# Steps moved off VectorE in a four-layer kernel, and the ranks of its order set anew

## What is computed

```python
# 1: selective scan, 256 channels, 32 states
delta = softplus(x @ W_bc[:64].T @ W_dt.T + b_dt);  B, C = x @ W_bc[64:96].T, x @ W_bc[96:].T
h[t] = exp(delta[t] * A) * h[t-1] + delta[t] * x[t] * B[t];   y[t] = sum_n h[t] * C[t] + D * x[t]
# 2: dense FFN, 704 hidden, weights (wq - 128) * scale
y = (silu(x @ Wg.T) * (x @ Wu.T)) @ Wd.T
# 3: convolution of 4 taps and scan, 512 channels, 16 states
hs = silu(conv4(x @ W_in.T) + conv_b);  delta = softplus((hs @ W_dt.T) @ W_dtproj.T + b)
y = (scan(hs, delta, B, C) + D * hs) * silu(x @ W_gate.T) @ W_out.T
# 4: causal attention, 16 heads of 128; experts, the best 6 of 16, and a shared one
x4 = x + softmax(q k^T / sqrt(128) + mask) v @ wo          # q, k, v from rmsnorm(x) * ln1
y  = x4 - x + sum_e cw[e] * (silu(h @ eg[e].T) * (h @ eu[e].T)) @ ed[e].T + shared(h)  # h: rmsnorm(x4) * ln2
```

## Time and profile before

| | us |
|---|---|
| median of 3 runs | 1362.71 |
| lowest, highest | 1359.16, 1363.14 |
| profiled execution, its own time | 1363.67 |
| its span, first to last instruction | 1362.4 |
| PE, DVE busy | 1119.7, 1030.9 |
| ACT, POOL busy | 596.2, 600.4 |

### The profile page before, as it was taken

One profiled execution on the slowest core, in us unless ns is written; L12 is line 12 of the kernel. 1 busy time (PEld: TensorE's weight loads), 2 busy tenths in 40 slices (PEclk: granted clock), 3 DMA queues, 4 the chain that ended last, 5 costly groups with the idle time before them and its releaser, 6 DMA issues. The chain is left out here.

```text
span 1362.4 us, 17002 instructions
## 1 busy us (share of the span) xinstructions
PE 1119.7 (82%) x5224; PEld 879.8 (65%) x5224; DVE 1030.9 (76%) x1879; ACT 596.2 (44%) x1543; POOL 600.4 (44%) x487
## 2 busy tenths in 40 slices
PE   4557536499695899977977899799998999999797
PEld 2335324377584678755855787587877877777586
DVE  5797899989999999999997885699944444444433
ACT  4553555454664336555753232565532123333210
POOL 3577477964575687654875640176600000000000
PEclk9798758899797999998988999899999999999899
DMA  4652124353254775433765641266543643222173
GB/s 135 251 195 74 48 88 142 108 158 105 85 174 155 218 232 166 136 101 111 210 216 156 196 144 43 83 201 199 162 144 104 204 136 104 95 93 81 58 210 103
DMA packets 105434, 191.54 MB, mean 141 GB/s; under 512 B 11648, under 2 KB 42368, under 8 KB 105088
## 3 DMA queue, kind: packets, MB, share of 16 engines
q1 hardware_dynamic: 91520, 177.42, 41.9%
q10 hardware_dynamic: 13824, 13.05, 3.1%
HBM read 176.33 MB, written 14.09 MB: 140 GB/s over the span
## 5 line engine op out<-in xcount | busy, mean ns | idle before, releaser
L1957 DVE TENSOR_TENSOR_SCAN scan_banks<-scan_banks,h_end,drive 128x256 f32<-128x256 f32 x480 | 338.5, 742 | 13.9 <-POOL drive L2291 11.0
L2321 POOL TENSOR_TENSOR sum<-sum,state 128x512 f32<-128x512 f32 x174 | 227.3, 1306 | 54.4 <-DVE state L1969 52.3
L2291 POOL TENSOR_TENSOR drive<-w0T,bc_rows 128x512 f32<-128x512 f32 x128 | 164.3, 1291 | 152.0 <-DVE scan_banks L1957 98.0
L2291 POOL TENSOR_TENSOR drive<-w1T,bc_rows 128x512 f32<-128x512 f32 x128 | 163.4, 1283 | 139.6 <-DVE scan_banks L1957 61.4
L2324 POOL TENSOR_TENSOR stats_b<-stats_b,neg_half 128x2 f32<-128x2 f32 x12 | 8.8, 732 | 367.4 <-DVE stats_b L2129 200.8
L1969 DVE TENSOR_TENSOR state<-scan_banks,bc_rows 128x512 f32<-128x512 f32 x240 | 162.7, 678 | 0.6
L1410 PE MATMUL score_banks<-state,ident 128*128 128x256 f32 x256 | 85.2, 483 | 79.3 <-DVE state L1969 44.7
L1560 PE MATMUL score_banks<-kv,qT 128*128 128x512 f32 (+3 forms) x360 | 135.7, 493 | 6.4 <-ACT probs L1865 3.7
L2144 DVE TENSOR_REDUCE soft<-score_banks 128x1 f32<-128x128 f32 (+4 forms) x122 | 88.0, 729 | 61.9 <-PE score_banks L1562 61.6
L1865 ACT ACTIVATE probs<-score_banks,soft 128x128 f32<-128x128 f32 (+4 forms) x122 | 87.8, 721 | 97.5 <-DVE soft L2144 96.7
L1410 PEld LDWEIGHTS score_banks<-state,ident 128*128 128x128 f32 x256 | 57.2, 239 | 107.5 <-DVE state L1969 57.4
(11 more groups left out here) (203 smaller groups left out, 2098.6 us busy)
## 6 DMA issues: line engine op xcount, KB each, us to landing
bc_rows<-bc_rows SPq DMA_DIRECT2D x256, 256.0 KB, 3.8
streamed_w<-in_w_head SPq DMA_DIRECT2D x64, 384.0 KB, 5.0
expert_w<-in_w_moe SPq DMA_DIRECT2D x52, 384.0 KB, 4.4
kv_past<-kv ACTq DMA_DIRECT2D x48, 256.0 KB, 3.2
kv<-in_w_moe SPq DMA_DIRECT2D x32, 384.0 KB, 3.9
kv<-kv_past SPq DMA_DIRECT2D x16, 768.0 KB, 4.7
kv<-kv_past SPq DMA_DIRECT2D x16, 512.0 KB, 5.0
streamed_w<-in_w_moe SPq DMA_DIRECT2D x16, 384.0 KB, 4.1
```

Source lines behind the costliest of these rows:

```text
L1957: done = e.engine.tensor_tensor_scan(states, decays, drive[g % len(drive)][:, i, 0:size], h_end[layer][:, n, kt:kt + 1], ALU.mult, ALU.add)
L2291: self.tt(drive[g % len(drive)][:, :, 0:size], w_of(layer, c)[:, PAIR * half:PAIR * (half + 1), 0:size], rows_of(g, c, 0), ALU.mult).then_ ...
L2321: self.tt(to, so_far, slot_of(c, layer, k), ALU.add).then_inc(added, 1)
```

## The change

Parts of stages are handed to other engines, and the planner's numbers are new.

- `softplus_sum` keeps two instructions on DVE (minimum and last sum). cs, e - cs and plus max(x, 0) go to POOL (`softplus_rest`), `w` too (`delta_x`). `softplus_log` is split into `softplus_exp` and `softplus_log`. The half in layer 1's `w` goes into the weights that make B (scale 0.25 for 0.5).
- The first tap of the convolution goes from DVE to ACT, 16 instructions in all; `rms_scale` goes from DVE to ACT, 16.
- `weigh_up` of chunks 0 and 1 goes from DVE to POOL, 22 instructions.
- `on_scalar`: all groups of chunks 0 and 1, and groups 0 and 2 of chunk 2 are copied by ACT (before: group 1 of each); chunk 3 as before.
- The costs of `pe`, `pe_turn` and of transfers, the lags, `EARLIER` and the lanes' ranks are new, and with them the order on every engine.

```diff
-    return "pe", sum(0.018 + 0.00172 * n for n in columns)
+    return "pe", sum(0.012 + 0.00169 * n for n in columns)
-DMA = "sp", 0.3
+def dma(kilobytes):
+    return "sp", max(0.5, kilobytes / 230)
...
-        return [Lane(self.fetches(), 0.00, 1), Lane(self.decays(), 0.60), Lane(self.drives(), 0.30), Lane(self.scans(), 0.10),
+        return [Lane(self.fetches(), 2.10, 1), Lane(self.decays(), 0.70), Lane(self.drives(), 0.10), Lane(self.scans(), -0.80),
...
-    return j == 2 if c == LAST else j % 2 == 1
+    return j == 2 if c == LAST else c < 2 or j != 1
...
             def softplus_sum(self, c, g):
-                self.ts(cs, es, 1.0, -1.0, ALU.add, ALU.add).then_inc(*self.order.tick())
+                e.wait_ge(sp_one[layer], c, half)
                 e.wait_ge(sp_ln[layer], c, half)
-                self.settle()
                 self.tt(ls, ls, cs, ALU.min).then_inc(*self.order.tick())
-                self.tt(cs, es, cs, ALU.subtract).then_inc(*self.order.tick())
-                self.tt(cs, cs, xs, ALU.add).then_inc(*self.order.tick())
+                e.wait_ge(sp_rest[layer], c, half)
-                self.tt(to, cs, ls, ALU.add).then_inc(delta_ready[layer].sem, 1)
-                    self.stt(to_w, hs[:, 2 * half:2 * half + 2, 0:size], 0.5, to, ALU.mult,
-                             ALU.mult).then_inc(w_ready[1].sem, 1)
-                    self.tt(to_w, to, x0s[c % 2][:, :, 0:size], ALU.mult).then_inc(w_ready[0].sem, 1)
+                self.tt(to, lost, ls, ALU.add).then_inc(delta_ready[layer].sem, 1)
...
+            def softplus_rest(self, c, g):                       # GpSimd
+                e.wait_ge(sp_exp[layer], c, half)
+                self.ts(cs, es, 1.0, -1.0, ALU.add, ALU.add).then_inc(sp_one[layer].sem, 1)
+                e.wait_ge(sp_one[layer], c, half)
+                wait_unit(e, driven, c - 1 if layer else c - 2, layer)
+                self.tt(lost, es, cs, ALU.subtract).then_inc(sp_lost[layer].sem, 1)
+                e.wait_ge(sp_lost[layer], c, half)
+                e.wait_ge(sp_x[layer], c, 2 * half + 1)
+                self.tt(lost, lost, xs, ALU.add).then_inc(sp_rest[layer].sem, 1)
+            def delta_x(self, c, g):                             # GpSimd
+                e.wait_ge(delta_ready[layer], c, half)
+                self.tt(to, of, x, ALU.mult).then_inc(w_ready[layer].sem, 1)
...
+            def conv_taps(self, c, kt):                          # ScalarE
+                self.activation(hs[:, kt, 0:size], pad_hs[:, kt, 0:size], ACT.Identity, bias=col("conv_b", kt),
+                                scale=col("conv_w", kt * TAPS)).then_inc(conv_begun.sem, 1)
...
+            def rms_scale(self, c, r):                           # ScalarE
+                    done = self.activation(hn[:, tb, :], x[:, tb, :], ACT.Copy, scale=st[:, tb, 2:3])
...
+            def weigh_up(self, c, g):                            # GpSimd, c < WEIGHED_BY_POOL = 2
+                self.tt(by_tile(to, size), by_tile(to, size), cw_rows[cw_at(c, r)][:, 0:len(GROUPS[g]), 0:size],
+                        ALU.mult).then_inc(moe_weighed.sem, 1)
```

More of the change, by code:

```diff
@@ L170, in nothing @@
         pass
-    load = load_x = dbc = project_dt = softplus_abs = softplus_x = softplus_log = softplus_sum = chore = nothing
+    load = load_x = dbc = project_dt = softplus_abs = softplus_x = softplus_exp = softplus_rest = softplus_log = softplus_sum = delta_x = chore = nothing
     fetch = decay = drive = scan = weigh = carry = add_up = skip0 = skip1 = nothing
@@ L298, in fetches @@
             after = ((f"rows{layer}", c),) + ((("weigh", g - ROWS),) if g >= ROWS else ())
-            yield Stage(partial(self.p.fetch, g, c, layer, k), (DMA,), after, (("rows", g),), lag=3.0)
+            yield Stage(partial(self.p.fetch, g, c, layer, k), (dma(SIZES[c]),), after, (("rows", g),), lag=2.4)
     def each(self):
@@ L328, in drives @@
             g, c, layer, k = unit
-            after = [("delta", c, 0 if layer == 0 else 1 + k // STATE1), ("rows", g)]
+            after = [("w", c, 0 if layer == 0 else 1 + k // STATE1), ("rows", g)]
             if g >= DRIVES:
@@ L415, in lanes @@
     def lanes(self):
-        return [Lane(self.first(), 0.20, 8), Lane(self.second(), 1.30, 16)]
+        return [Lane(self.first(), -0.30, 8), Lane(self.second(), 1.00, 16)]
     def softplus(self, c, g, given, use):
@@ L519, in load_lane @@
     for i in range(len(LOADS)):
-        yield Stage(partial(p.load, i), (DMA,), (("scan", i + 1),), (("in", i),), lag=10.0)
+        yield Stage(partial(p.load, i), (dma(LOADED_KB[i]),), (("scan", 2 * i + 1),), (("in", i),), lag=4.0)
 def chore_lane(p):
@@ L536, in lanes @@
     def lanes(self):
-        return [Lane(self.into_heads(), 0.60, 8), Lane(self.projections(), 0.60, 8), Lane(self.scores(), 1.00, 6),
-                Lane(self.products(), 1.10, 8), Lane(self.results(), 1.10, 8), Lane(self.experts(), 2.50, 2),
-                Lane(self.routing(), 1.50, 8), Lane(self.weights(), 2.20, 2),
-                Lane(self.hidden(), 1.20, 6),
-                Lane(self.weighed(), 1.90, 4), Lane(self.sums(), 1.80, 6)]
+        return [Lane(self.into_heads(), 0.40, 8), Lane(self.projections(), 0.90, 8), Lane(self.scores(), 1.20, 6),
+                Lane(self.products(), 1.00, 8), Lane(self.results(), 2.50, 8), Lane(self.experts(), 2.50, 2),
+                Lane(self.routing(), 2.50, 8), Lane(self.weights(), 2.00, 2),
+                Lane(self.hidden(), 2.50, 6),
+                Lane(self.weighed(), 1.00, 4), Lane(self.sums(), 2.50, 6)]
     def rms(self, c, r, given):
@@ L669, in experts @@
                     after = (("qk_mm", c, HEADS - 4 + LENT), ("v_mm", c, HEADS - 4 + LENT))
-                yield Stage(partial(p.fetch_expert, c, n), (DMA,), after, (("expert", c, n),), lag=4.5)
+                yield Stage(partial(p.fetch_expert, c, n), (dma(3 * DIM * P / 256),), after, (("expert", c, n),), lag=2.4)
     def routing(self):
@@ L1681, in chore @@
                     e.wait_value(mamba_in, MAMBA_IN)
-                    self.activation(w_x1[:, :, :], w_x1[:, :, :], ACT.Copy, scale=0.5).then_inc(adjusted.sem, 1)
+                    for lo, hi, scale in ((0, P, 0.5), (P, P + STATE1, 0.25), (P + STATE1, P + 2 * STATE1, 0.5)):
+                        columns_ = w_x1[:, :, lo:hi]
+                        self.activation(columns_, columns_, ACT.Copy, scale=scale).then_inc(adjusted.sem, 1)
             def decay(self, g, c, layer, k):
@@ L1740, in softplus_abs, with softplus_exp @@
                                     bias=col(name, 2 * half + k)).then_inc(sp_abs[layer].sem, 1)
+            def softplus_exp(self, c, g):
+                e, es, layer, half = self.e, hid[:, 2:4, 0:SIZES[c]], min(g, 1), max(g - 1, 0)
+                e.wait_ge(sp_abs[layer], c, 2 * half + 1)
+                self.activation(es, es, ACT.Exp, scale=-1.0).then_inc(sp_exp[layer].sem, 1)
             def softplus_log(self, c, g):
@@ L1744, in softplus_log @@
                 es, ls = hid[:, 2:4, 0:size], hid[:, 4:6, 0:size]
-                e.wait_ge(sp_abs[layer], c, 2 * half + 1)
-                self.activation(es, es, ACT.Exp, scale=-1.0).then_inc(sp_exp[layer].sem, 1)
                 e.wait_ge(sp_exp[layer], c, half)
@@ L1814, in rms_square @@
                 done.then_inc(squared[r].sem, 1)
+            def rms_scale(self, c, r):
+                e, st, x, n = self.e, stats_b[r], (x3[c % 2], x4)[r], blocks(c)
+                e.wait_ge(rms_ready[r], c)
+                for tb in range(n):
+                    done = self.activation(hn[:, tb, :], x[:, tb, :], ACT.Copy, scale=st[:, tb, 2:3])
+                done.then_inc(rms_scaled[r].sem, 1)
             def rms_turn(self, c, r):
@@ L2084, in conv_taps @@
                 e, size = self.e, SIZES[c]
[L2085 to L2088 removed]
+                e.wait_ge(conv_begun, c, kt)
                 for j in range(1, TAPS):
@@ L2283, in __init__ @@
             def __init__(self, e):
-                self.e, self.tt = e, e.engine.tensor_tensor
+                self.e, self.tt, self.ts = e, e.engine.tensor_tensor, e.engine.tensor_scalar
             def drive(self, g, c, layer, k):
```

104 lines of the change are left out of this document (59 added, 45 removed).

## The result

The changed kernel takes 1351.5 us (median of 5, 1347.3 to 1355.1) against 1361.1 us for the kernel before in the same comparison (1359.2 to 1363.1). The ratio is 0.9928, 95% interval 0.9901 to 0.9956: faster, but by 10 us where I had forecast 40. The profiled execution of after, 1347.3 us, lies 4 us under its median; that of before lay 2.6 us over. So some 7 us of the 16 us between the two traces is scatter.

The account below looks back on a forecast made before the run. DVE was taken to bound the kernel up to the 448th scan, PE after it. 799 - 77 + 5 = 727, 185 + 32 = 217 and 378, plus 1.3, made 1323 us; likeliest case 1305 to 1342, whole range 1289 to 1352.

Parts of the forecast that it names:

- A: Stretch up to the 448th scan, taken as DVE's: 799 us before, forecast 727.
- B: Stretch from the 448th to the last scan, taken as PE's: 185 us before, forecast 217.
- C: Stretch behind the last scan, taken as PE's: forecast unchanged at 378 us.
- the late groups: Six expert groups of chunk 1 moved behind the 448th scan: 5.3 us of PE each, 32 us in all.
- rival 1: Behind the 448th scan, late expert groups cost nothing because PE fills its idle time: 1291 us, chance 0.14.
- What leaves DVE: 182 instructions of 107.2 us leave DVE; 91 us real after overlap, 77 before the 448th scan.
- rival 4: Copies and steps left on DVE take longer, by 21 us: 1344 us; upper edge of the sum's 0.58.
- rival 2: Before the 448th scan, time doesn't shrink with DVE: half turned into waiting 1361 us, a third 1349; chance 0.18.
- my signs: Marks of rival 2: 448th scan after 760 us, with DVE under 85% busy before it.
- POOL's work at 5 us: Before the 448th scan, softplus delays from POOL's list lose 5 us, within 0 to 31.
- rival 3: GpSimd's list becomes the bound before the 448th scan: 1408 us if all delays scans, deciding from 45 us; chance 0.10.
- ACT at 0: Copies, taps and scales moved to ACT, at most 50 us, taken as hidden behind DVE's work: cost 0.

Follow-up runs that it names:

- first experiment: Kernel before in its own order, 167 of the moved DVE instructions cut to one column, nothing added on any engine: ratio 0.9829, 1336.6 us.

## Why the prediction was right and wrong

- **What bounds the stretches: right.** A follows DVE in part, B and C follow PE in the main. C came within 1 us of the forecast, and B within 2, so the price of the late groups (32 us) and the rejection of rival 1 held. The last scan came at 967, not near 910. B isn't PE's alone: it fell from 219 to 211 us without POOL's new work.
- **What leaves DVE: right, a little short.** 80 us of 91 in all, 71 of 77 in A. Of the missing 11 us, 8 are the final sum of softplus, 12 times 17.0 us in all where it was 9.2; the minimum got 3 us cheaper in turn (15.3 to 12.3). That is rival 4 at a net 5 us, and I had priced it at nothing.
- **The step that failed: "A shrinks by 77 us if DVE stays its bound and its idle 84 us stay", with a loss of 5.** They did not stay: A shrank by 51 us, and its idle time was 103 us. Relief alone raised idle time from 84 to 101 us in the first experiment, with no work added anywhere; 0.4 of the relief turned into waiting. That is rival 2's mechanism, and I gave it 0.18 because DVE was 90% busy; the other 10% were not a constant, but grew as DVE had less to do. Its price for a third of the 77 us was 1349, and 1351.5 is the measurement, but that is luck in part: in after idle time grew by little more than a quarter of the relief, and the rest of the miss is POOL's. Of my signs (the 448th scan after 760 us, DVE under 85% busy before it) neither came: it was 748 us and 86%.
- **POOL's work at 5 us: wrong.** "It isn't a bound by its sum" was true (78% in 268 to 748, from 63%) and didn't answer the question. With 64 us of it left out, 24 us came back, 12 of them in A in the traces, two thirds of these as shorter DVE instructions (8 us). It is rival 3's mechanism in part, far under its 45 us. Of the terms: the one-input step 1.94 us where I took 1.29 and bounded by 1.31; an undelayed softplus 1.6 us longer than before where I had 0.3; and the slow final sums above. They came about by the overlap with POOL's drives and sums that the minimum had paid before; I had taken it that the minimum alone would go on paying it.
- **ACT at 0: not tested by itself.** Its prices were higher than mine, 0.593 and 0.500 for the tap and the scale against 0.416. ACT is busy 59% in 268 to 748, and DVE's waits for its decays come to 5.3 us in A, from 1.6 before. That "DVE hardly waits for ACT in A" holds for the decays only: all its waits for ACT there were 21 us before and are 27 now.
- **How the 21 us in A split.** Without most of POOL's new work A is 735 us: 12 us of the 21 are POOL's. The other 8 to 9 are in the main idle time that grew beyond the 5 us that I had put for it. Each of these numbers comes from one trace and carries the 7 us named above. What DVE waits for when it has less to do can be read in part. Its waits in A, summed by the engine that ended them (us):

| kernel | PE | ACT | POOL |
|---|---|---|---|
| before | 32 | 21 | 18 |
| first experiment | 42 | 25 | 20 |
| after | 42 | 27 | 23 |
| without most of POOL's new work | 44 | 26 | 19 |

  More than half of what relief alone added is waiting for PE, and little of it for POOL, where my rival 2 named the loop through scan banks and drives. Whether PE is full in places there or only comes late in a chain stays open, since the run that thinned PE's work relieved it by 4.5 us in A.
- **The ends of my likeliest range don't follow from its terms.** A loss in A of 0 to 31 for the 5, and 10 us either way, give 1308 to 1359 and not 1305 to 1342. Added up rightly, the sum's own case reaches past 1351.5; its middle was still 28 us off.

## What to carry to other kernels

A bound engine's idle time is not a constant of the stretch. Here DVE was 90% busy before the 448th scan, and of the work taken off it 0.5 to 0.9 came back as time, 0.6 where nothing else changed; forecast with a range, and test with the work left out and put nowhere. An engine with slack by its sum is not free when its instructions stand in the loop of the bound engine; here 64 us on an engine busy 78% cost 24. And after a move, look at what ends up behind the last step of the long chain: the moves were 1.7% slower than before with the old order and 0.7% faster with the new one, and 1.8% faster with two of them trimmed and a third order.
